# Multiplying a whole unit of values (512 queries) in every second step of an attention loop, in place of half a unit (256 queries) in each

## The reference

```python
x = x + _pos_encoding(S, d, yellow)[None, :, :]
Q, K, V = (proj(Wq, bq), proj(Wk, bk), proj(Wv, bv))     # 16 heads of 8 channels
logits = jnp.einsum('bhqd,bhkd->bhqk', Q, K) / scale
attn = jax.nn.softmax(logits * scale_matrix, axis=-1)
out = jnp.einsum('bhqk,bhkd->bhqd', attn, V) * (1.0 + yellow * eps_adaptive)
```

## Time and profile before

| | us |
|---|---|
| median of 3 executions (2806.03 to 2818.52) | 2807.62 |
| the profiled execution, its own time | 2809.47 |
| its span in the profile, first to last instruction | 2807.6 |

### The profile page before, as it was taken

How to read it: one execution, slowest core, us unless ns; L and a number is a source line. 1 busy time by engine, 2 the same in 40 slices (tenths; PEclk the granted TensorE clock), 3 DMA queues, 4 the chain that set the end, 5 groups by cost and what they waited for, 6 DMA issues and landing times.

```text
span 2807.6 us, 46582 instructions
## 1 busy us (share of the span) xinstructions
PE 2203.1 (78%) x17520; PEld 1250.1 (45%) x17520; DVE 2017.1 (72%) x4264; ACT 1425.9 (51%) x2581; POOL 559.2 (20%) x336
## 2 busy tenths in 40 slices
PE   4799388877879848878679956887877993888777
PEld 4567212354647512236455731234564761223545
DVE  4864589778674569967777549967877556996777
ACT  1334157674633327756553424776473341675745
POOL 0153000124043200030406210003313430002140
PEclk9999679989979859999889977998988995999888
DMA  4000210001000020010100020001100002001010
GB/s 143 0 1 1 68 24 10 18 18 30 12 9 1 1 80 17 10 29 5 29 20 1 1 68 13 19 7 29 23 15 16 1 1 80 17 7 26 10 29 19
DMA packets 50228, 63.88 MB, mean 23 GB/s; under 512 B 16160, under 2 KB 27680, under 8 KB 49472
## 3 DMA queue, kind: packets, MB, share of 16 engines
q1 hardware_dynamic: 46792, 54.87, 7.7%
q10 hardware_dynamic: 3192, 5.80, 0.7%
HBM read 25.19 MB, written 15.01 MB: 14 GB/s over the span
## 4 chain that ended last, share of the span: by engine, by line
PE 48%; DVE 28%; ACT 12%; issue 6%; DMA 3%; SPq 2%; POOL 0%; ACTq 0%; DVEq 0%; POOLq 0%
PE PS L1261 44%; DVE arena L1015 10%; ACT arena L638 6%; DVE arena L1116 2%; ACT arena L585 2%; PE PS L1559 1%; PE PS L1279 1%; DVE s_at L1091 1%; DMA scr_k<-arena 1%; DVE arena L1121 1%; DVE arena L1084 1%; DMA arena<-scr_k 1%; DMA tmp<-xf 1%; DVE tmp L1091 1%; DVE arena L1202 1%
## 5 line engine op out<-in xcount | busy, mean ns | idle before, releaser
L1261 PE MATMUL PS<-arena 128*32 128x256 f32 (+4 forms) x10240 | 819.1, 352 | 205.0 <-DMA arena<-scr_k 75.6
L1015 DVE TENSOR_REDUCE arena<-PS 128x1 f32<-128x512 f32 x1024 | 641.8, 684 | 97.9 <-PE PS L1261 97.8
L585 ACT ACTIVATE arena<-PS 128x1024 f32<-128x1024 f32 x512 | 517.2, 1031 | 306.8 <-PE PS L1261 306.8
L1261 PEld LDWEIGHTS PS<-arena 128*32 128x32 f32 (+4 forms) x10240 | 311.3, 122 | 707.8 <-DVE arena L1015 280.2
L541 ACT ACTIVATE arena<-PS 128x512 f32<-128x512 f32 x256 | 150.7, 597 | 245.6 <-PE PS L1261 245.4
L1261 PEld LDWEIGHTS PS<-w2e,arena 128*128 128x128 f32 x2048 | 246.0, 192 | 51.7 <-issue 51.7
L1261 PE MATMUL PS<-w2e,arena 128*128 128x128 f32 x2048 | 246.7, 275 | 0.0
L638 ACT ACTIVATE arena<-PS,arena 128x128 f32<-128x128 f32 x512 | 230.8, 549 | 21.4 <-DVE arena L1152 20.1
L961 DVE TENSOR_TENSOR arena<-PS,arena 128x512 f32<-128x512 f32 x128 | 86.1, 689 | 213.7 <-PE PS L1261 213.3
L1261 PE MATMUL PS<-wqkv,arena 128*128 128x512 f32 x384 | 185.5, 625 | 24.9 <-ACT arena L620 21.7
L430 POOL TENSOR_TENSOR zz<-zz,arena 128x512 f32<-128x512 f32 x104 | 133.6, 1285 | 270.9 <-DVE arena L961 242.9
(11 more groups left out here) (298 smaller groups left out, 3478.2 us busy)
## 6 DMA issues: line engine op xcount, KB each, us to landing
arena<-arena SPq DMA_DIRECT2D x120, 128.0 KB, 2.3
arena<-scr_k SPq DMA_DIRECT2D x28, 200.0 KB
arena<-scr_q SPq DMA_DIRECT2D x28, 192.0 KB
scr_q<-arena SPq DMA_DIRECT2D x16, 256.0 KB, 3.1
scr_k<-arena SPq DMA_DIRECT2D x16, 256.0 KB, 5.3
x_in<-in_x SPq DMA_DIRECT2D x5, 512.0 KB, 4.0
scr_q<-arena ACTq DMA_DIRECT2D x8, 256.0 KB, 5.0
scr_k<-arena ACTq DMA_DIRECT2D x8, 256.0 KB, 5.9
```

Of the source, the lines that this page charges most:

```text
L585: act.activation(pb[:, n % 8], pair(2 * (n % 2)), ACT.Exp).then_inc(S["p"], 1)
L1015: dve.tensor_reduce(mxp[:, h % 2, j, t, hf:hf + 1], PS[:, ring_bank("mx", h, n), :], AX, ALU.max)\
L1261: return pe.matmul(o, w, v, start=start, stop=stop, **kw)
```

## The change

In the steps from 3 on, the values are issued in odd steps alone, and for all 512 queries: four matmuls (eight in the profile) of 512 columns in place of four of 256 in this step and four of 256 in the next. The semaphore `S["pv"]`, which counts finished units for ScalarE, is raised at the end of the odd step in place of the even one behind it. Even steps have only maxima and scores.

```diff
-                    if n >= 3:
-                        u, i = (n - 3) // 2, (n - 3) % 2
+                    if n >= 3 and n % 2 == 1:
+                        u = (n - 3) // 2
                         h, k = u // T, u % T
-                        if i == 0:
-                            pe.wait_ge(S["p"], 2 * u + 2)
-                        if k == 0 and i == 0 and h:
+                        pe.wait_ge(S["p"], 2 * u + 2)
+                        if k == 0 and h:
                             pe.wait_ge(S["on"], h)
                         for j in range(GH):
-                            c = HALF * (j % 2) + HALF // 2 * i
-                            ins = mm(PS[32 * j:32 * j + 32, 4, HALF // 2 * i:HALF // 2 * i + HALF // 2],
-                                     vaug[:, k, GH * (h // 2) + j], pb[:, (2 * u + j // 2) % 8, c:c + HALF // 2],
-                                     start=(k == 0 and i == 0), stop=(k == T - 1), tile_position=(0, 32 * j),
-                                     skip_group_check=True)
-                        if i == 1:
-                            ins.then_inc(S["pv"], 1)
+                            c = HALF * (j % 2)
+                            ins = mm(PS[32 * j:32 * j + 32, 4, :], vaug[:, k, GH * (h // 2) + j],
+                                     pb[:, (2 * u + j // 2) % 8, c:c + HALF], start=(k == 0), stop=(k == T - 1),
+                                     tile_position=(0, 32 * j), skip_group_check=True)
+                        ins.then_inc(S["pv"], 1)
```

## The result

The changed kernel takes 2907.02 us (median of 4 executions, 2898.15 to 2911.53) against 2809.74 us (4 executions, 2806.03 to 2818.52): a ratio of 1.0338, 95% interval 1.0301 to 1.0374. It is slower by 97 us, where the forecast was 86. The profiled execution is the shortest of the four: 2898.15 us, span 2896.3 us, mean granted clock 0.885; the other three had 0.880 or 0.881. Its span is 88.7 us above that of before.

The account below looks back on a forecast made before the run. A closed loop of VectorE and TensorE over three banks was taken to bound the kernel. Late pairs 67, steps without maxima 3 and clock 16 gave 86 us, 2893.6 us against the median, range 2855 to 2940.

Parts of the forecast that it names:

- What bounds the stage: Steps with maxima: VectorE and TensorE form a closed loop over three banks, 1.25 us a step; lateness is not made up.
- The pair of steps: Odd step 1.60 us plus even step 1.23 is 2.83 against 2.50: +0.33 us, 204 times, +67 us.
- the step whose values wait for the copy: Exception where the bank 4 copy holds values up: slack already gone, so the whole 0.43 us of added columns shows.
- The steps without maxima: 23 steps a batch, set by ScalarE: some 0.15 us more in four steps, 0.8 us a batch, +3 us.
- The clock: Even steps leave TensorE idle, so the clock rises later: 12 us a batch more at 1.2 GHz, +16 us.
- The sum: 67 + 3 + 16 = 86 us: profiled execution 2809.5 to 2895.5 us, median 2893.6 us, 3.1% slower.
- A: Rival, steps with maxima: TensorE's throughput sets the pace; two steps 2.03 us, 63 us less, 2744 us; chance 0.05.
- B: Rival, steps with maxima: VectorE makes the late pair up, so no change, 2811 us; chance 0.08.
- C: Rival: clock stays at 1.2 GHz for two passes a batch or falls again, 61 us more, 2950 us; chance 0.12.
- A sign that was named wrongly: In the profile, loads for maxima behind an odd step's values wait for issue, those of even steps for line 1015.
- The other signs: Two steps 2.83 us; VectorE idle 0.3 us before every second pair, about 20 us in all; value matmuls about 600 ns.
- The saved change between row and column strips: Even step: by the drain rule alone two steps 0.3 us shorter, but hidden where TensorE waits for VectorE.

Follow-up runs that it names:

- short-reduction run: Each reduction on line 1015 reads 64 of its 512 columns: 2691.08 us in the kernel before, 2706.94 us in the changed kernel.
- filled runs: Changed kernel, even steps' score matmuls repeated: twice 2897.72 us, three times 2904.69, three times only with maxima 2887.42; three times with 256 value columns 2838.97, with 384 2857.26.

## Why the prediction was right

Point by point, by its own steps:

- **What bounds the stage: right.** The loop of VectorE and TensorE over three banks, with lateness added in full and never made up. With 256, 384 and 512 columns two steps take 2.49, 2.59 and 2.80 us; with one more result in store part of it is made up; with a short reduction the pair's loss falls from 0.30 to 0.11 us.
- **The pair of steps: +0.33 forecast, +0.30 measured.** The odd step is 1.56, not 1.60 us: the 0.60 from the earlier trace rows held 0.03 of a load that had run ahead, the engine's own need is 0.57 (446.79 to 447.36 in the short-reduction run of the kernel before), and the columns cost 0.42, not 0.43 (the odd step's second part is now 461.25 - 460.26 = 0.99). The even step is 1.24, against 1.23. So the slack in the step of before was 0.14 and not 0.08. 204 x 0.30 = 61 us, where the forecast had 67. In the step whose values wait for the copy the columns show nearly whole, as said: from the load at 442.54 to that at 445.84 it is 3.30 us, against 460.50 - 457.61 = 2.89 before. At 1.2 GHz the two steps of the changed kernel are 4.31 us (loads for maxima at 408.15, 409.60 and 412.46), where the forecast had 4.30.
- **The steps without maxima: right in size.** Between the exponentials of steps 105 and 127 it is 22.97 us in three of the four batches, against 22.16 or 22.17: 0.8 us a batch; in the fourth batch there is no difference, so it is some 2 to 3 us. The 0.03 us that the sum adds for ScalarE's own semaphore stands on no row, and no run shows it by itself; without it the term would be 0.12 us in four steps, not 0.15.
- **The clock: +16 forecast, about 17 in the profiled execution.** Its stages spent some 60 us more at 1.2 GHz, 15 a batch, where I took 12. They are 84 us longer; 65 of these are the passes and some 2 the steps without maxima, which leaves 17 for the clock; by the forecast's 0.34 for each us it would be 20. A pass of the changed kernel in which the clock fell for 6.8 us took 26.5 us in place of 24.3, 0.32 for each. That filling the even steps raises the clock is shown by the filled runs. That it falls because the even steps are thin, as the forecast had it, is argued: the short-reduction runs, where the changed kernel has the higher clock, show that this is not all of it. In which batch it stays low is not forecast by anything here.
- **The sum.** In the profiled execution it is 61 (pairs), 4 (turns of the passes, which the forecast had called small), some 2, 17 and 4.7 us outside the stages, not taken apart: 89 us, 2898.15 against the 2895.5 forecast from 2809.5. That this is so close is in part luck: the pairs were 6 us too dear in the forecast, and the turns and the time outside the stages, which it left out, make up for that. The median is 9 us longer than this execution, and its clock is lower (0.880 or 0.881 against 0.885), so most of the difference between 86 and 97 is the clock: of the median's 97 us some 70 are not clock, and some 25 are.
- **A and B** fell: A by the pair of steps, 2.80 us and not 2.03, and even with short reductions 2.33 against 2.22, since the loop's 0.77 us is still above the even step's own work; B by VectorE's idle 0.23 to 0.26 us before each second pair. **C** came about in small part at 512 columns (in the second and third batch the clock fell again for 6.8 us in each of two later passes). With 256 columns it was worse than C: 0.52 or 0.53 in all four stages.
- **A sign that was named wrongly.** I had said that loads behind an odd step's values would be shown as waiting for issue. They are put down to VectorE's line 1015, with 0.84 us; only VectorE's own idle time shows which of the two was late. The other signs came as named: 2.80 us for two steps, 610 ns for a value matmul, and idle time of 0.107 us for each reduction, which for the 179 of the earlier trace rows is 19 us, where I had said about 20.

The saved change between row and column strips brought nothing. Of this case's 0.57 us from the load for the values to the next, 0.14 are left beside two rounds of 0.215; in the even step, where the change was saved, 1.24 us of loop lie over it. The Trainium skill, page "TensorEngine Tiling (Array Packing)", section "Key Properties", has each change of tiling mode drain the engine. No run here shows whether the 0.14 us are such a drain, since none leaves the change of strips out where TensorE sets the pace.

## What to carry to other kernels

Where two engines pass work back and forth over a small ring of buffers, the turn of that loop is a deadline for every single step, and work that is moved from one step to the next is free up to the slack and paid in full above it, however idle the lighter step is, unless the loop has something in store: one result more took the late pair from 0.30 to 0.21 us. Before asking how much work an engine has, ask whether it can run ahead: here, one wait placed in front of the instruction that needs it, and not in front of the pair, was worth 0.6%. And taking work from TensorE can cost more than it saves, by way of its clock (2999 us with half the value work, against 2907), so compare the clocks of two runs before their totals.

## What was not expected of the hardware

- Leaving out half the value work of the changed kernel made it 92 us slower (2907 to 2999 us), with a granted clock of 0.52 to 0.53 in all four stages; 0.43 us of repeated matmuls in every second step brought it back to 0.87 and 2839 us.
- Eight float32 matmuls of 256 columns with their sixteen loads take as long as four of 512 with eight: 1.57 us against 1.56 in the odd step.
- With short reductions TensorE was busy for 162.95 of 176.50 us of the first stage before the change and for 147.77 of 176.10 after it, and the granted clock was 0.89 in the first and 0.96 in the second.
- The same kernel's executions differ by the clock that they happen to be granted: 2898.15 us at a mean of 0.885, 2904 to 2912 us at 0.880 or 0.881.
